# First attention: two parts of the second unit's scores move into the values step, on the upper rows of TensorE

## The reference, cut to what matters

```python
q = (x @ Wq.T + bq).reshape(B, S, H, HD).transpose(0, 2, 1, 3)
k = (x @ Wk.T + bk).reshape(B, S, HK, HD).transpose(0, 2, 1, 3)
v = (x @ Wv.T + bv).reshape(B, S, HK, HD).transpose(0, 2, 1, 3)
k, v = jnp.repeat(k, G, axis=1), jnp.repeat(v, G, axis=1)
scores = jnp.einsum('bhqd,bhkd->bhqk', q, k) * scale
allowed = (qi >= kj) & (qi - kj < WINDOW)
scores = jnp.where(allowed[None, None], scores, neg)
logits = jnp.concatenate([scores, sink], axis=-1)
probs = jax.nn.softmax(logits, axis=-1)[..., :-1]
o = jnp.einsum('bhqk,bhkd->bhqd', probs, v)
o = o.transpose(0, 2, 1, 3).reshape(B, S, H * HD)
return o @ Wo.T + bo
```

## Time and profile before

| | |
|---|---|
| median of 3 runs | 3861.61 us |
| profiled execution, its own time | 3860.01 us |
| its span | 3858.2 us |
| mean granted TensorE clock | 0.946 of full |
| PE, DVE, ACT, POOL busy | 91%, 79%, 58%, 37% of the span |
| TensorE clock from 66 to 1370 us, the 128 groups | 1.00 |

### The profile page before, as it was taken

One profiled execution on the slowest core, in us unless ns is written; L12 is line 12 of the kernel. 1 busy time (PEld: TensorE's weight loads), 2 busy tenths in 40 slices (PEclk: granted clock), 3 DMA queues, 4 the chain that ended last, 5 costly groups with the idle time before them and its releaser, 6 DMA issues.

```text
span 3858.2 us, 93855 instructions
## 1 busy us (share of the span) xinstructions
PE 3529.1 (91%) x32894; PEld 2469.3 (64%) x32894; DVE 3049.2 (79%) x11272; ACT 2231.2 (58%) x6991; POOL 1442.1 (37%) x1741
## 2 busy tenths in 40 slices
PE   7999999999999989899989969989878999899855
PEld 6888888888888866666644433335555666555542
DVE  7888888888988866677779967767886778888771
ACT  5888888898888842267654434433333222477611
POOL 2555555545555510145448845520000000222117
PEclk9999999999999989889989989999988999899958
DMA  3000000000000012210000000000000000000023
GB/s 130 3 3 3 3 3 3 3 3 3 3 3 3 3 59 87 62 67 2 2 0 1 0 11 0 1 1 1 1 1 34 1 1 1 34 2 2 23 61 49
DMA packets 30897, 64.58 MB, mean 17 GB/s; under 512 B 3424, under 2 KB 19808, under 8 KB 29152
## 3 DMA queue, kind: packets, MB, share of 16 engines
q1 hardware_dynamic: 24288, 52.29, 3.9%
q0 software_dynamic: 6144, 6.30, 1.0%
HBM read 49.93 MB, written 8.65 MB: 15 GB/s over the span
## 4 chain that ended last, share of the span: by engine, by line
PE 69%; DVE 17%; ACT 5%; issue 5%; POOL 2%; DMA 1%; DVEq 0%; POOLq 0%; ACTq 0%; SPq 0%
PE ps L176 9%; PE ps L536 8%; PE ps L496 7%; PE ps L473 6%; PE ps L520 6%; PE ps L1679 3%; PE ps L1650 3%; PE ps L1648 3%; PE ps L2303 3%; PE ps L2290 2%; DVE gbbc L2342 2%; PE ps L1019 2%; DVE gbbc L2331 2%; DVE gbbc L2337 2%; PE ps L983 2%
## 5 line engine op out<-in xcount | busy, mean ns | idle before, releaser
L741 ACT ACTIVATE T<-T 128x128 f32<-128x128 f32 x1024 | 396.9, 397 | 8.9 <-DVE T L662 8.9
L741 ACT ACTIVATE W<-T 128x128 f32<-128x128 f32 x1024 | 397.2, 399 | 1.3 <-DVE T L662 1.3
L642 DVE CUSTOM_DVE_ANT_0 T<-ps,C 128x128 f32<-128x128 f32 x1536 | 381.3, 286 | 0.0
L652 DVE COPY_PREDICATED W<-gbbc,ps 128x512 f32<-128x512 int32 x512 | 342.7, 722 | 3.2 <-PE ps L176 2.6
L536 PE MATMUL ps<-W,gbbc 64*64 64x128 f32 (+1 forms) x6912 | 316.4, 311 | 2.1 <-DVE W L652 1.2
L496 PE MATMUL ps<-T 64*64 64x192 f32 (+2 forms) x8192 | 313.3, 290 | 4.2 <-DVE T L642 4.1
L176 PE MATMUL ps<-C,T 128*128 128x128 f32 (+1 forms) x1620 | 262.1, 298 | 49.8 <-DVE T L307 18.9
L496 PEld LDWEIGHTS ps<-T 64*64 64x64 f32 x8192 | 254.5, 133 | 77.9 <-issue 45.5
L1246 POOL TENSOR_TENSOR QK<-T,QK 128x512 fp32r<-128x512 f32 x128 | 161.9, 1274 | 376.2 <-ACT T L1206 258.1
L536 PEld LDWEIGHTS ps<-W,gbbc 64*64 64x64 f32 x6912 | 280.2, 133 | 24.9 <-PE ps L536 19.3
L832 POOL TENSOR_TENSOR W<-W,T 128x512 f32<-128x512 f32 x256 | 260.8, 1040 | 78.1 <-DVE T L669 78.1
(11 more groups left out here) (420 smaller groups left out, 8782.9 us busy)
## 6 DMA issues: line engine op xcount, KB each, us to landing
T<-crow_dram SPq DMA_DIRECT2D x128, 128.0 KB, 3.0
W<-in_l1f_dram SPq DMA_DIRECT2D x1, 6152.0 KB, 18.2
W<-in_l0a_dram SPq DMA_DIRECT2D x1, 5172.5 KB, 25.6
W<-in_l2f_dram SPq DMA_DIRECT2D x1, 3160.0 KB, 10.5
W<-in_l3f_dram SPq DMA_DIRECT2D x1, 3076.0 KB, 10.0
W<-in_sm_dram SPq DMA_DIRECT2D x1, 2729.0 KB, 9.2
W<-in_l0f_dram SPq DMA_DIRECT2D x1, 2256.0 KB, 30.4
X<-in_x_dram SPq DMA_DIRECT2D x1, 2048.0 KB, 7.4
```

The costliest lines, as they stand in the source:

```text
L642: done(e.tensor_tensor_reduce(sm[:, at:at + 128], src, m, 1.0, -3.0e38, ALU.add, ALU.max, mx[:, col:col + 1]), s["masked"], x == (3 if ban ...
L652: e.copy_predicated(a.PT[t % 2][:, 512 + 512 * j:1024 + 512 * j].rearrange("p (h w) -> p h w", h=4), is_.unsqueeze(1).broadcast_to([P, 4, ...
L741: done(e.activation(a.Pr[i % 4][:, at:at + w_], a.Sm[i % 2][:, at:at + w_], ACT.Exp, bias=a.ngs[i % 4][:, c:c + 1], scale=a.scale, accum_o ...
```

## The change

`scores` takes the list of parts to do. Where a group's values stand between the two units' scores, parts (1, 1, 0) and (1, 1, 1) of unit 2n+1, both on the upper rows, are issued inside `values`: the first ahead of the wait for `beats`, the second ahead of the wait for `ebbs`. The other six parts stay where the eight were. Within `values`, the lower rows' first piece in unit j after `ebbs` changes place with the upper rows' piece in unit i. On DVE, bank 1 is masked right behind its own merge and ahead of bank 0's merge, and the two parts wait for that bank alone (3i - 2). The amount of work is the same on every engine.

```diff
+    FIRST = (0, 0, 0), (1, 1, 0), (0, 0, 1), (1, 1, 1), (0, 1, 0), (1, 0, 0), (0, 1, 1), (1, 0, 1)
+    REST = (0, 0, 0), (0, 0, 1), (0, 1, 0), (1, 0, 0), (0, 1, 1), (1, 0, 1)
-    def scores(i):
+    def scores(i, parts=FIRST):
-        past(e, s["masked"], 3 * i - 1)
-        for p, qt, j in ((0, 0, 0), (1, 1, 0), (0, 0, 1), (1, 1, 1), (0, 1, 0), (1, 0, 0), (0, 1, 1), (1, 0, 1)):
+        past(e, s["masked"], 3 * i - (1 if (0, 0, 0) in parts else 2))
+        for p, qt, j in parts:
...
-    def values(n):
+    def values(n, beside):
...
         piece(j, 2, high, (1,), "beats")
         piece(i, 1, low, (0,), "ebbs")
+        if beside is not None:
+            scores(beside, ((1, 1, 0),))
         e.wait_ge(*s["beats"](n + 1))
         piece(j, 2, low, (0, 1))
+        if beside is not None:
+            scores(beside, ((1, 1, 1),))
         e.wait_ge(*s["ebbs"](n + 1))
+        piece(j, 1, low, (0,))
         piece(i, 1, high, (0, 1))
-        piece(j, 1, low, (0,))
         piece(i, 0, high, (1,))
...
-            values(leaving)
+            values(leaving, None if n is None else 2 * n + 1)
         if n is not None:
-            scores(2 * n + 1)
+            scores(2 * n + 1, FIRST if leaving is None else REST)
...
         merge(i, 1)
+        mask(i, 1)
         merge(i, 0)
-        mask(i, 1)
         mask(i, 2)
         mask(i, 0)
```

## The result

The changed kernel takes 3893.3 us (median of 11 runs, 3887.4 to 3917.8) against 3861.0 (11 runs, 3856.1 to 3888.1). The ratio is 1.0082, with a 95% interval of 1.0065 to 1.0099: slower, by less than 1%. The forecast was 3886 us. The profiled execution takes 3889.4 us against 3860.0, 29.4 more.

A forecast was written before the change was run, and what follows sets the result against it. PE was taken to bound each round; 96 rounds x 0.17 us (16.3) and 30 x 0.27 (8.1) add 24.4 us, giving 3886 us (+0.6%), within 1%. The range was 3857 to 3912.

The forecast's parts named there:

- What bounds the kernel: In the stretch from 66 to 1370 us PE bounds each round: busy 1301 of 1304 us at full clock.
- No gain from filled upper tiles: Values and second scores: 384 columns move within the upper rows, lower rows keep 1280 + 576; gain costed at zero.
- The new wait: Part (1, 1, 0) waits for DVE's mask of bank 1: load at 602.24, multiplications from 602.29, directly costing lower rows nothing.
- The rival with the late mask: DVE's merge and mask of bank 1: mask later than worked out, run slower by over 1%; chance 0.2.
- The queue: End of the values: a waiting upper piece stops PE's intake for all tiles; lower rows lose 0.17 us a round.
- The deeper intake: PE takes in more than one waiting matmul per tile, so lower rows lose nothing: 3862 us; chance 0.2.
- Strict order of loads: Alternative intake rule on PE: a load only once the tile's weights are free; played through, ends the stretch 0.06 us late.
- The mis-sized term: The lower rows' loss to PE's intake in the values: 0.17 us a plain round, net 0.27 in rounds behind `stats`.
- Off the path: ACT's later copy of the outputs (0.42 covered by 0.50 us) and DVE's added 0.12 us (0.59 cover) cost nothing.

The follow-up runs named there:

- the mask in time: The changed kernel with bank 1's merge left out on DVE, so that its mask is done 0.46 us earlier: ratio 0.9997.
- The experiment with the old order: The changed kernel with DVE's old order, both merges and then the mask of bank 1: ratio 1.0151.
- the order of five pieces alone: The kernel before with the three upper pieces of the values' first five handed in ahead of the two lower ones: ratio 1.0138.

## Why the prediction was right

**What bounds the kernel.** Right: PE's records and clock are the same, each microsecond of a longer round is the kernel's.

**No gain from filled upper tiles.** Right. With the mask in time (part at 1.98 us) the plain round is not shorter than before, although 384 columns have left the second scores; the lower rows' 1856 columns stay.

**The new wait.** Right in each link: gap of the dependent pair 0.04 us (0.03 taken), read to load 0.12 (0.11 taken), load of the part 2.11 us into the round (2.11 forecast). The rival with the late mask needed a gap of 0.14 and has 0.04. The experiment with the old order shows what that rival would have cost: it is over 1%.

**The queue.** The rule is right, shown by the order of five pieces alone (+0.42 us with no semaphore in play), by one-for-one growth with the part's start, and by the fall to 0.085 when the lower pieces are handed in first. The deeper intake, with a chance of 0.2, is excluded. Strict order of loads is too: in the change the lower rows' last piece loads at 3.29 us, ahead of the upper piece that stands before it in the program, which loads at 3.36.

**The mis-sized term.** 0.17 us in a plain round; measured 0.21. I followed one pair of upper tiles, the first column half. The intake stands still until the upper tiles of both column halves have started their piece of part 0 in unit i, and the second half's starts 0.035 us later: 3.25 and 3.29 us into the round by the single records. Then the lower rows' last piece loads (3.29 and 3.30) and multiplies at 3.35; before it did so at 3.13 to 3.14, which is 0.21. In the rounds behind `stats` the same 0.04 is missing, 0.31 against 0.27. Together 126 x 0.04 = 5 us, the whole difference between the 24.4 us predicted and the 29.4 between the profiled executions. The medians of the runs are 32 us apart, the interval 25 to 38; both sums lie near it, the measured one inside, the predicted one just under its lower end.

How little gets in during that stop is seen in the windows of 0.12 us, first after the change, where the upper piece is waited for:

```profile
609.21:609.33 0.12, 0.12 (x8) 0.08 (x2) 0.12 (x3) 0.00 (x0) 0.12 (x1) 1.00 0.47 137
```

and before, near the same point of the values:

```profile
603.13:603.25 0.12, 0.12 (x14) 0.12 (x8) 0.12 (x3) 0.00 (x0) 0.00 (x0) 1.00 0.00 0
```

Two loads instead of eight. PE counts as busy in both: a stopped intake does not show as idle time while the other tiles still multiply. It shows in the count of loads. The transfers in the first window (0.47 of the DMA engines, 137 GB/s) are not the reason: DMA has 0.01 over the whole stretch, and all 78 plain rounds within a batch take 10.43 to 10.45 us.

Two slips of arithmetic did no harm. Twice 0.82 ns is 1.64, not 1.66, and the records show 1.69: those of 192 columns start 162 ns apart. That makes the upper chain's 640 columns 0.02 us longer and the lower chain's 512 columns 0.015, so it nearly cancels. And the rival of the deeper intake reaches down to 3857 with its 30 x 0.16 us, not to 3855.

**Off the path.** Right, and as narrow as forecast: ACT's idle time ahead of the query projection is 0.11 us (0.1 forecast), DVE keeps 0.50 us of its wait. The mask of bank 2 is read 0.13 us later (0.12 forecast) and still ahead of the lower rows' scores.

## What to carry to other kernels

Where PE works on several tiles at once, count columns for each tile first: work moved onto idle tiles was worth nothing here, since the fullest tiles kept their own. Then look at the program order: a piece that waits for its tile, or for a mask, also stops the loads of tiles that are free, so hand in the fuller half's pieces ahead of the emptier half's late ones (0.085 us a round lost instead of 0.21). When following such a queue, follow every tile, since the last of them opens it.

## What was not expected

**The first two rounds differ from run to run.** Windows of 44 to 66 us, before the rounds run at full clock (the last but two number is the granted clock), of the kernel before:

```profile
44.00:66.00 22.00, 15.72 (x203) 12.54 (x203) 17.16 (x92) 13.34 (x63) 7.01 (x14) 0.86 0.00 1
```

of the changed kernel:

```profile
44.00:66.00 22.00, 16.47 (x151) 12.03 (x150) 14.59 (x85) 9.14 (x45) 6.01 (x12) 0.58 0.00 1
```

and of the one with the exchange alone, which does in these rounds what the kernel before does:

```profile
44.00:66.00 22.00, 15.72 (x230) 11.87 (x233) 18.22 (x102) 14.76 (x70) 8.26 (x15) 0.96 0.01 1
```

PE is idle for a quarter of these windows or more (15.72 to 16.47 of 22 us busy). The mean granted clock lies between 0.55 and 0.98 over the eleven profiled executions; the first values multiply at 65.9 us before, 70.2 after, and from 63.5 to 70.2 in the experiments, in no order that fits the edits. That is 6.7 us between the earliest and the latest. What follows the last group's values differs as well, from 2484.9 to 2495.3 us over the same eleven. A comparison of two single profiles as wholes holds both; the per-round figures and the first to last values don't.

**An earlier end that nothing follows.** The load that waits for `beats` goes out at the same moment when the matmul it is taken to wait for is done 0.06 us earlier. This stays open. In the prediction's sum that wait was the same before and after, so nothing hung on it.
